# Decoder layer on one core: another deal of maxima, projections and context loads over the beats of the cross-attention

## The chip, the core and the metric

One core of one Trainium2 chip runs the kernel. The metric is the device time of one execution in microseconds; lower is better. TensorE (PE) does the matrix products and transposes, VectorE (DVE) the reductions and most element-wise work, ScalarE (ACT) exponentials and copies, GpSimd (POOL) sums and some DMA issues, SyncE (SP) only DMA issues.

## The reference, cut to what matters

`x` is 8 x 224 x 512, the context 8 x 750 x 512, all in float32. Three sublayers follow each other, each on the layer norm of the stream and added to it.

```
x = x + attn(layernorm(x), Wq, Wk, Wv, Wo, G1, G2, gamma, beta, theta)   # linear, causal, gated
x = x + xattn(layernorm(x), ctx, w_q, w_kv, w_proj, w_rel)
x = x + ffn(layernorm(x), w_gate, w_up, w_down)                          # ternary weights

# xattn: 16 heads of 32
q = x_q @ w_q ; k, v = split(ctx @ w_kv)
logits = q k^T * 32**-0.5 + (query position - key position) * w_rel[head]
out = softmax(logits) v  -> joined heads @ w_proj
```

The change touches the cross-attention alone.

## The kernel before, in words

The three sublayers run one after another: `self_attention`, `cross_attention`, `ternary_ffn`. Each engine has its own instruction stream, all written out in Python loops; semaphores join them. Engines take their instructions strictly in the order written, so the schedule is what the lists below say.

In `cross_attention` (L779) a batch has four slots, `s` = 0 to 3, one for each group of four heads. A slot has 16 beats `k`. What each engine does in a beat is written in fixed order:

- TensorE (L1371 to L1386): the maxima halves of the beat (`maxima_half`, L1311), at beat 12 `turn_maxima` (L1326), then the logits of a unit in beats 0 to 11 (`logits`, L1297: four heads for each of three pairs of key blocks), in beats 5, 9 and 13 a product with the values (`attend`, L1333), at beat 2 the denominators of the slot before (L1350), and last a part of a filler (`do`, L1235).
- Maxima: for the next slot (`n` is its number over all batches), each of 4 heads x 2 halves of the queries x 2 halves of the keys (376 columns) is one matmul into `psM`, which has two banks; VectorE reduces it (`reduce_half`, L1169). Half h goes to bank h % 2, so TensorE waits at half h for the reduction of half h - 2. After the last half VectorE joins them (`join_maxima`, L1179, at beat 11); TensorE turns the result at beat 12 and ScalarE copies it as the shift into `q4` (`take_shift`, L1089). `halves_at` (L806) says which halves lie in which beat: here 16 in beats 0 to 10.
- Fillers (`fill`, L815): projections and transposes that the slot has room for. K{g}a and K{g}b are the two halves of the keys of head group g, in three parts of four matmuls over three beats each; V{t} the values of key block t and Y{t} the output projection, three parts each; q{g} queries, r{t} the transposes of context block t, and Xa, Xb the transposes of x, in one beat each. Y belongs to the batch before, K2 and K3 to the batch itself, all others to the next one. V takes 12 matmuls of 512 columns, K 12 of 376, q 12 of 224, r and X four transposes.
- Each filler writes one of the two banks of `psR`, in turn (`bank_of`, L846 to L856, by the order of all fillers). The first part of a filler waits until the bank's filler before it has been read. Reading (`take` of ScalarE, L1061, and of VectorE, L1138) is put at the beat after a filler has ended: for K, r, X and q ScalarE copies the rounded high part and VectorE then subtracts it for the low part; V is only copied, Y only added. In VectorE's stream a beat's reductions stand ahead of its `take`, and at beat 2 both stand ahead of `divide` (L1183: reciprocal and product).
- SyncE packs keys and queries from `k_st` and `q_st` into `k4` and `q4` with DMAs (`pack_keys`, L932, 12 of them; `pack_queries`, L944). Keys of a group go over a buffer that the logits two slots earlier still read, so their four heads are packed behind beats 8 to 11. `k_st` is single: the copy of the next K{g}a (L1071) waits until all of the group before has been packed. The order of all this is fixed at L966 to L976.
- GpSimd, for each slot (L1036 to L1048): `split_heads` of the slot before (L996), in slot 0 of batches 1 to 6 the load of the next context (`load_context`, L1023, 1.5 MB by its own DMA queue), `store` in slot 1, `sum_keys` (L1008, five additions of 125 x 896 behind the exponentials), then `clear_shift` (L983). The context b goes into `cv[:, b % 2]` once the values of batch b - 2 have been used up (`pv_done`).

The kernel has two further pieces that matter for bounds: logits go to three banks, so the logits of a unit wait for the exponential of three units earlier (L1303), and all r of a batch must have been read before its K0a begins (L1244).

Of the kernel before, what the change touches and what calls it, by code (L numbers as in the profile page):

```python
# [19 lines left out]
NG = D // P  # L20
# [21 lines left out]
def wait_count(eng, sem, value):  # L42

    if not (isinstance(value, int) and value <= 0):
        eng.wait_ge(sem, value)


def wait_apart(eng, sem, value, passed):

    eng.wait_ge(sem, value)  # L50
    eng.sem_inc(passed, 1)
# [727 lines left out]
def cross_attention(nc, sems, x1, ctx_rows, k_rows, q_rows, x2, shared):  # L779
# [5 lines left out]
    B, N, _ = x1.shape  # L785
# [17 lines left out]
    BEATS = 16  # L803


    halves_at = [range(0, 1), range(1, 2), range(2, 4), range(4, 5), range(5, 7), range(7, 8), range(8, 10),  # L806
                 range(10, 11), range(11, 13), range(13, 14), range(14, 16)] + [range(0)] * 5
    unit_at = [(k // HG, k % HG) if k < UNITS else None for k in range(BEATS)]
    attend_at = {5: 0, 9: 1, 13: 2}
    DENOMINATORS_AT = 2  # L810
# [2 lines left out]

    parts_of = {"V": 3, "K": 3, "Y": 3, "q": 1, "r": 1, "X": 1}
    fill = [  # L815
# [4 lines left out]
    ]  # L820
    first_fill = ["r0", "r1", "r2", "r3", "r4", "r5", "K0a", "K0b", "Xa", "Xb", "q0", "q1", "K1a", "K1b", "q2", "q3"]
# [29 lines left out]
    bank_of, use_of, high_of = {}, {}, {}  # L851
# [6 lines left out]
    with ExitStack() as ctx:  # L858
# [42 lines left out]
        read = [sem("read_A"), sem("read_B")]  # L901
# [76 lines left out]
        @block.gpsimd  # L978
        def _(pool):
            nc.gpsimd.memset(eps_half[:], -0.5).then_inc(const_made, 1)  # L980
            pool.wait_ge(const_made, 1)

            def clear_shift(b, s):  # L983

                wait_apart(pool, st_full, UNITS * (NG * b + s + 1), pool_passed)
                nc.gpsimd.memset(q4[ROW_SHIFT:ROW_SHIFT + HG, s].bitcast(F32), 0.0).then_inc(shift_cleared, 1)
                pool.wait_ge(shift_cleared, NG * b + s + 1)

            def rstd(b):
                wait_apart(pool, x_meanvar, NT * (b + 1), pool_passed)  # L990
                nc.gpsimd.tensor_scalar(x_ve[:], x_mv[:, :, 1], EPS, None, ALU.add).then_inc(x_veps, 1)
                pool.wait_ge(x_veps, b + 1)
                nc.gpsimd.tensor_tensor(x_rs[:], x_ve[:], eps_half[:], ALU.pow).then_inc(x_rstd, 1)
                pool.wait_ge(x_rstd, b + 1)

            def split_heads(b, s):  # L996

                n = NG * b + s
                if s == 0 and b >= 1:
                    for what in ("Y0", "Y1"):  # L1000
                        wait_apart(pool, full[bank_of[what, b - 1]], use_of[what, b - 1], pool_passed)
                wait_apart(pool, o_ready, n + 1, pool_passed)
                nc.gpsimd.tensor_scalar(oT_hi[:, s], o_f[:], 1.0, None, ALU.mult).then_inc(oT_hi_ready, 1)  # L1003
                pool.wait_ge(oT_hi_ready, n + 1)
                nc.gpsimd.tensor_tensor(oT_lo[:, s], o_f[:], oT_hi[:, s].bitcast(F32), ALU.subtract).then_inc(oT_ready, 1)
                pool.wait_ge(oT_ready, n + 1)

            def sum_keys(b, s):  # L1008

                n = NG * b + s  # L1010
                wait_count(pool, den_full, n)
                for m in range(SUMS):
                    i, a = divmod(m + 1, 2)
                    tile = pT[:, (s + i) % 2, :, a * N:(a + 1) * N]
                    if m in (0, 1, 3):
                        wait_apart(pool, exp_done, UNITS * n + HG * (i + 1), pool_passed)
                    before = pT[:, s % 2, :, 0:N] if m == 0 else p_sum[:]
                    if m > 0:
                        pool.wait_ge(p_summed, SUMS * n + m)
                    nc.gpsimd.tensor_tensor(p_sum[:], before, tile, ALU.add).then_inc(p_summed, 1)  # L1020
                pool.wait_ge(p_summed, SUMS * (n + 1))

            def load_context(b):  # L1023

                wait_count(pool, pv_done, NB * NG * (b - 1))
                pool.dma_start(cv[:, b % 2], ctx_rows[b].rearrange("(a p) d -> p a d", p=KB)).then_inc(c_in, DMA)

            def store(b):
                for what in ("Y0", "Y1"):
                    pool.wait_ge(read[bank_of[what, b]], use_of[what, b])  # L1030
                pool.dma_start(x2_rows[b], x_res[:]).then_inc(stored, DMA)

            rstd(0)
            load_context(1)
            rstd(1)
            for b in range(B):  # L1036
                for s in range(NG):
                    if (b, s) != (0, 0):
                        split_heads(*((b, s - 1) if s > 0 else (b - 1, NG - 1)))
                    if s == 0 and b >= 1 and b + 1 < B:  # L1040
                        load_context(b + 1)
                    if s == 1 and b >= 1:
                        store(b - 1)
                    if s == 3 and b + 2 < B:
                        rstd(b + 2)
                    sum_keys(b, s)
                    if b + 1 < B:
                        clear_shift(b, s)  # L1048
            split_heads(B - 1, NG - 1)
            store(B - 1)  # L1050
            pool.wait_ge(stored, B * DMA)
# [180 lines left out]
        def _(pe):  # L1232
            M = nc.tensor

            def do(what, b, part):  # L1235

                r = bank_of[what, b]
# [4 lines left out]
                if what[0] == "K":  # L1242
                    g, seg = int(what[1]), "ab".index(what[2])
                    if g == 0 and seg == 0 and part == 0:  # L1244
                        for t in range(NK):
                            pe.wait_ge(read[bank_of[f"r{t}", b]], use_of[f"r{t}", b])
                    lo = seg * (S - SEG)
                    out = out[:, 0:SEG]
                    left = lambda i, k: (w_hi, w_lo)[i][:, 1, k, g * P:(g + 1) * P]
                    right = lambda i, k: (cT_hi, cT_lo)[i][:, k, lo:lo + SEG]  # L1250
                elif what[0] == "r":
                    t = int(what[1])
                    if t == 0:
                        wait_count(pe, c_in, DMA * b)
                    for k in range(KT):
                        last = M.transpose(out[:, k * KB:(k + 1) * KB], cv[:, b % 2, t, k * P:(k + 1) * P], ident[0:KB, 0:KB])
                    last.then_inc(full[r], 1)
                    return
                elif what[0] == "X":
                    seg = "ab".index(what[1])  # L1260
                    if seg == 0:
                        pe.wait_ge(xn_ready, NT * (b + 1))
                    for k in (0, 1):
                        for t in range(NT):
                            last = M.transpose(out[:, k * N + t * T:k * N + (t + 1) * T],
                                               xn[:, t, (2 * seg + k) * P:(2 * seg + k + 1) * P], ident[0:T, 0:T])
                    last.then_inc(full[r], 1)
                    return
                elif what[0] == "q":
                    g = int(what[1])  # L1270
                    for x_half in ("Xa", "Xb"):
                        pe.wait_ge(read[bank_of[x_half, b]], use_of[x_half, b])
                    out = out[:, 0:N]
                    left = lambda i, k: (w_hi, w_lo)[i][:, 0, k, g * P:(g + 1) * P]
                    right = lambda i, k: (xT_hi, xT_lo)[i][:, k, :]
                elif what[0] == "V":
                    t = int(what[1])
                    out = out[0:KB, :]
                    left = lambda i, k: (cT_hi, cT_lo)[i][:, k, t * KB:(t + 1) * KB]
                    right = lambda i, k: (w_hi, w_lo)[i][:, 2, k, :]  # L1280
                else:
                    t = int(what[1])
                    if part == 0:
                        pe.wait_ge(w_split_lo, 2)
                        pe.wait_ge(oT_ready, NG * (b + 1))
                    out = out[0:T, :]
                    left = lambda i, k: (oT_hi, oT_lo)[i][:, k, t * T:(t + 1) * T]
                    right = lambda i, k: (w_hi, w_lo)[i][:, 3, k, :]
                terms = [(i, j, k) for k in range(KT) for i, j in ((0, 0), (0, 1), (1, 0))]
                each = len(terms) // parts  # L1290
                for m in range(part * each, (part + 1) * each):
                    i, j, k = terms[m]
# [71 lines left out]
            for part in range(3):  # L1364
                do("V0", 0, part)
# [540 lines left out]
```

## Time and profile before

| | us |
|---|---|
| three runs | 1378.21, 1381.65, 2889.5 |
| their median | 1381.65 |
| the profiled execution | 1378.97 |
| its span, first to last instruction | 1377.4 |
| self-attention with its lead-in, from the start | 341.1 |
| cross-attention, from there to about | 1135 |

The profiled execution spends 1.57 us outside its span. The third of the three runs is far above the others and has no counterpart in the profile. The sections of the span were read from the first instruction of the cross-attention (341.10) and its last products (1128.56 and on).

In the timelines below a matmul's duration reaches past the start of the next one, since matmuls are pipelined; the distance between starts is what one takes of TensorE. Idle time in brackets is counted from the modelled end of the instruction before. Batches and slots are counted from 0.

### The profile page before, as it was taken

What the parts mean: (1) busy time and instruction counts of PE and PEld (TensorE: products, weight loads), DVE (VectorE), ACT (ScalarE), POOL (GpSimd) and SP (SyncE); (2) the same over time, 40 slices, a digit from 0 to 9 for tenths busy, and PEclk for the clock granted to TensorE, in tenths of its full rate; (3) what the DMA queues carried; (4) which work ended last, traced back from release to release, by engine and by line L of the source; (5) the groups of instructions that cost most, each with busy time, mean ns of one, the idle gap of its engine ahead of it and who ended that gap; (6) DMA issues with size and microseconds to landing.
All of it is one profiled execution on the core that took longest, in us unless ns stands there. A gap on an engine that the chain in (4) does not pass through costs nothing. (4 is left out here: it accounts for less than half of the span.)

```text
span 1377.4 us, 24731 instructions
## 1 busy us (share of the span) xinstructions
PE 1198.6 (87%) x9295; PEld 915.0 (66%) x9322; DVE 821.0 (60%) x1522; ACT 590.6 (43%) x955; POOL 515.8 (37%) x411
## 2 busy tenths in 40 slices
PE   4799989994689998999999989999999863599997
PEld 3687868882577777777777777777777643344443
DVE  5767646654356646465656465565654616688884
ACT  2222222231235444444444444454444324577775
POOL 0011111114006565656565646555655651001110
PEclk9899999997699999999999999999999855999999
DMA  5222242224413243344252532442423208212211
GB/s 159 87 74 86 77 139 96 82 90 137 124 47 102 51 131 94 77 118 101 63 144 55 126 102 68 118 105 60 120 74 87 61 0 327 84 54 69 69 61 38
DMA packets 72362, 129.42 MB, mean 94 GB/s; under 512 B 18572, under 2 KB 30988, under 8 KB 71739
## 3 DMA queue, kind: packets, MB, share of 16 engines
q1 hardware_dynamic: 60595, 106.43, 27.5%
q0 software_dynamic: 11680, 21.81, 5.0%
q8 instruction: 57, 0.93, 0.3%
q14 instruction: 30, 0.25, 0.1%
HBM read 68.96 MB, written 11.22 MB: 58 GB/s over the span
## 5 line engine op out<-in xcount | busy, mean ns | idle before, releaser
L1177 DVE TENSOR_REDUCE xa_m_part<-xa_psM 112x1 f32<-112x376 f32 x512 | 265.4, 544 | 258.9 <-PE xa_psM L1323 257.6
L1020 POOL TENSOR_TENSOR xa_p_sum<-xa_p_sum,space 125x896 f32<-125x896 f32 x128 | 270.1, 2110 | 124.0 <-ACT space L1101 118.6
L1101 ACT ACTIVATE space<-xa_psS 125x448 f32<-125x448 f32 x384 | 207.1, 544 | 237.0 <-PE xa_psS L1307 228.5
L1323 PE MATMUL xa_psM<-xa_k,xa_q 104*112 104x376 f32 x512 | 162.7, 356 | 21.8 <-DVE xa_m_part L1177 20.4
L1307 PE MATMUL xa_psS<-xa_q,xa_k 104*125 104x224 f32 x768 | 147.9, 278 | 0.0
L1307 PEld LDWEIGHTS xa_psS<-xa_q,xa_k 104*125 104x125 f32 x768 | 140.8, 194 | 8.2 <-issue 1.4
L1323 PEld LDWEIGHTS xa_psM<-xa_k,xa_q 104*112 104x112 f32 x512 | 89.6, 178 | 46.8 <-DVE xa_m_part L1177 32.8
L1345 PE MATMUL xa_psO<-space,cv 125*32 125x224 f32 x1536 | 97.9, 375 | 1.8 <-ACT space L1101 1.1
L1293 PE MATMUL xa_psR<-xa_cT_hi,w_hi 128*128 128x376 f32 x256 | 87.5, 342 | 9.7 <-DVE xa_cT_lo L1167 9.7
L1293 PE MATMUL xa_psR<-xa_cT_hi,w_lo 128*128 128x376 f32 x256 | 93.0, 363 | 0.0
L1293 PE MATMUL xa_psR<-xa_cT_lo,w_hi 128*128 128x376 f32 x256 | 86.5, 338 | 0.0
L60 PE MATMUL sa_psR<-sa_xT_hi,w_hi 128*128 128x224 f32 x256 | 72.8, 284 | 11.1 <-DVE sa_xT_lo L456 11.1
L1003 POOL TENSOR_SCALAR xa_oT_hi<-xa_o_f 128x224 fp32r<-128x224 f32 x32 | 24.7, 772 | 149.3 <-DVE xa_o_f L1190 149.3
L1293 PE MATMUL xa_psR<-w_hi,xa_cT_hi 128*125 128x512 f32 x192 | 78.2, 407 | 0.0
L1020 POOL TENSOR_TENSOR xa_p_sum<-space 125x896 f32<-125x896 f32 x32 | 67.6, 2112 | 27.4 <-ACT space L1101 23.4
L1293 PE MATMUL xa_psR<-w_lo,xa_cT_hi 128*125 128x512 f32 x192 | 77.3, 402 | 0.0
L1293 PE MATMUL xa_psR<-w_hi,xa_cT_lo 128*125 128x512 f32 x192 | 75.7, 394 | 0.0
L60 PE MATMUL sa_psR<-sa_xT_lo,w_hi 128*128 128x224 f32 x256 | 71.0, 277 | 0.0
L60 PE MATMUL sa_psR<-sa_xT_hi,w_lo 128*128 128x224 f32 x256 | 70.8, 277 | 0.0
L1056 ACT ACTIVATE xa_k_st<-xa_psR 128x376 fp32r<-128x376 f32 x64 | 30.9, 484 | 87.5 <-PE xa_psR L1293 65.7
L1807 PE MATMUL ff_psG<-ff_gu_T,ff_xq_T 128*128 128x512 bf16 x210 | 54.9, 380 | 13.6 <-DVE ff_h L1685 11.0
L1543 POOL DMA_DIRECT2D out_dram<-ff_y x14 | 8.7, 622 | 151.0 <-DVE ff_y L1700 151.0
(200 smaller groups left out, 2646.8 us busy)
## 6 DMA issues: line engine op xcount, KB each, us to landing
xa_k<-xa_k_st SPq DMA_DIRECT2D x384, 94.0 KB, 2.2
xa_q<-xa_q_st SPq DMA_DIRECT2D x192, 56.0 KB, 2.0
cv<-in_ctx_dram POOLq DMA_DIRECT2D x7, 1500.0 KB, 23.2
cv<-in_L_ffn_w_gate_dram SPq DMA_DIRECT2D x8, 512.0 KB, 4.9
cv<-in_L_ffn_w_up_dram SPq DMA_DIRECT2D x8, 512.0 KB, 6.1
cv<-in_L_ffn_w_down_dram SPq DMA_DIRECT2D x8, 512.0 KB, 7.1
ff_w_raw<-in_L_ffn_w_gate_dram SPq DMA_DIRECT2D x4, 1024.0 KB, 9.2
ff_w_raw<-in_L_ffn_w_up_dram SPq DMA_DIRECT2D x4, 1024.0 KB, 14.0
```

The lines of the kernel that those rows point to most:

```text
L60: ins = nc.tensor.matmul(out, left(i, c), right(j, c), start=first and n == 0, stop=last and n == len(terms) - 1)
L1003: nc.gpsimd.tensor_scalar(oT_hi[:, s], o_f[:], 1.0, None, ALU.mult).then_inc(oT_hi_ready, 1)
L1020: nc.gpsimd.tensor_tensor(p_sum[:], before, tile, ALU.add).then_inc(p_summed, 1)
L1056: return nc.scalar.activation(out, in_, ACT.Copy, scale=scale)
L1101: nc.scalar.activation(pT[:, (s + i) % 2, j], psS[0:KB, (HG * i + j) % NB, 0:2 * N], ACT.Exp).then_inc(exp_done, 1)
L1177: V.tensor_reduce(m_part[:, seg, t, jj:jj + 1], psM[0:T, seg, 0:SEG], AX.X, ALU.max, negate=True).then_inc(mx_read, 1)
L1293: last = M.matmul(out, left(i, k), right(j, k), start=m == 0, stop=m == len(terms) - 1)
L1307: last = M.matmul(psS[0:KB, (HG * i + j) % NB, a * N:(a + 1) * N], k4[0:ROWS, s % 2, j, col:col + KB], q4[0:ROWS, s, j, :], start=True, st ...
L1323: M.matmul(psM[0:T, seg, 0:SEG], q4[0:ROWS, g, jj, t * T:(t + 1) * T], k4[0:ROWS, g % 2, jj, seg * SEG:(seg + 1) * SEG], start=True, stop= ...
L1345: last = M.matmul(psO[HD * j:HD * (j + 1), 0:N], cv[:, b % 2, t, h * HD:(h + 1) * HD], pT[:, (s + i) % 2, j, a * N:(a + 1) * N], start=t == 0,
L1543: pool.dma_start(out_rows[i], y[:]).then_inc(stored, DMA)
L1807: last = M.matmul(bank[:, c % 2], xq_T[:, k], gu_T[:, w, k, c * CW:(c + 1) * CW], start=k == 0, stop=k == KT - 1)
```

## The change

It has four parts.

1. The 16 halves are dealt over twelve beats, 2, 1, 1, 1, 1, 1, 1, 2, 2, 1, 2, 1, in place of eleven beats with 1, 1, 2, 1, 2, 1, 2, 1, 2, 1, 2. The last half then stands in beat 11, in the beat of `join_maxima` and right ahead of `turn_maxima`.
2. The fillers are dealt otherwise. Y0 and the two X change places in slot 0, Y1 moves from beat 13 to 11; q2, q3 go from slot 0 to slot 2; in slot 1 r and q alternate and V0 takes beats 12 to 14; r4 and r5 move to slot 1's last beat and slot 2's beat 1; K0 moves from beats 0 to 5 of slot 2 to beats 3 to 8. Slot 3 stays. All in all the same fillers run; the banks follow from the new order.
3. The context of batch b + 2 is asked for at the end of slot 3 of batch b, behind `clear_shift`, in place of slot 0 of batch b + 1 between `split_heads` and `sum_keys`. There are six such loads either way.
4. The first part of a V waits for r{t} of its block to have been read, one wait more in TensorE's stream for each V.

```diff
--- before.py
+++ after.py
@@ -803,8 +803,8 @@
     BEATS = 16
 
 
-    halves_at = [range(0, 1), range(1, 2), range(2, 4), range(4, 5), range(5, 7), range(7, 8), range(8, 10),
-                 range(10, 11), range(11, 13), range(13, 14), range(14, 16)] + [range(0)] * 5
+    counts = (2, 1, 1, 1, 1, 1, 1, 2, 2, 1, 2, 1)
+    halves_at = [range(sum(counts[:k]), sum(counts[:k + 1])) for k in range(BEATS)]
     unit_at = [(k // HG, k % HG) if k < UNITS else None for k in range(BEATS)]
     attend_at = {5: 0, 9: 1, 13: 2}
     DENOMINATORS_AT = 2
@@ -813,9 +813,9 @@
 
     parts_of = {"V": 3, "K": 3, "Y": 3, "q": 1, "r": 1, "X": 1}
     fill = [
-        {0: "K2a", 3: "K2b", 6: "Xa", 7: "Xb", 8: "Y0", 11: "q2", 12: "q3", 13: "Y1"},
-        {0: "K3a", 3: "K3b", 6: "r0", 7: "r1", 8: "q0", 9: "r2", 10: "r3", 11: "q1", 12: "r4", 13: "r5"},
-        {0: "K0a", 3: "K0b", 6: "V0", 9: "V1", 12: "V2"},
+        {0: "K2a", 3: "K2b", 6: "Y0", 9: "Xa", 10: "Xb", 11: "Y1"},
+        {0: "K3a", 3: "K3b", 6: "r0", 7: "q0", 8: "r1", 9: "q1", 10: "r2", 11: "r3", 12: "V0", 15: "r4"},
+        {0: "q2", 1: "r5", 2: "q3", 3: "K0a", 6: "K0b", 9: "V1", 12: "V2"},
         {0: "K1a", 3: "K1b", 6: "V3", 9: "V4", 12: "V5"},
     ]
     first_fill = ["r0", "r1", "r2", "r3", "r4", "r5", "K0a", "K0b", "Xa", "Xb", "q0", "q1", "K1a", "K1b", "q2", "q3"]
@@ -1037,8 +1037,6 @@
                 for s in range(NG):
                     if (b, s) != (0, 0):
                         split_heads(*((b, s - 1) if s > 0 else (b - 1, NG - 1)))
-                    if s == 0 and b >= 1 and b + 1 < B:
-                        load_context(b + 1)
                     if s == 1 and b >= 1:
                         store(b - 1)
                     if s == 3 and b + 2 < B:
@@ -1046,6 +1044,8 @@
                     sum_keys(b, s)
                     if b + 1 < B:
                         clear_shift(b, s)
+                    if s == NG - 1 and b + 2 < B:
+                        load_context(b + 2)
             split_heads(B - 1, NG - 1)
             store(B - 1)
             pool.wait_ge(stored, B * DMA)
@@ -1275,6 +1275,8 @@
                     right = lambda i, k: (xT_hi, xT_lo)[i][:, k, :]
                 elif what[0] == "V":
                     t = int(what[1])
+                    if part == 0:
+                        pe.wait_ge(read[bank_of[f"r{t}", b]], use_of[f"r{t}", b])
                     out = out[0:KB, :]
                     left = lambda i, k: (cT_hi, cT_lo)[i][:, k, t * KB:(t + 1) * KB]
                     right = lambda i, k: (w_hi, w_lo)[i][:, 2, k, :]
```

## Rows read from the trace of the kernel before

**Rows 1.** The page: TensorE's busy time, and its granted clock in 40 slices
```profile
PE 1198.6 (87%) x9295; PEld 915.0 (66%) x9322; DVE 821.0 (60%) x1522; ACT 590.6 (43%) x955; POOL 515.8 (37%) x411
...
PEclk9899999997699999999999999999999855999999
```

**Rows 2.** Stretches: two batches of the cross-attention, each from reciprocal to reciprocal
```profile
core 0: us, PE busy (x) PEld busy (x) DVE busy (x) ACT busy (x) POOL busy (x), PEclk, DMA share, GB/s
...
586.30:678.90 92.60, 88.13 (x665) 71.22 (x666) 53.64 (x105) 41.54 (x78) 54.68 (x36) 1.00 0.38 97
...
678.90:770.80 91.90, 87.94 (x665) 71.33 (x666) 53.62 (x106) 41.67 (x79) 54.69 (x36) 1.00 0.38 99
```

**Rows 3.** TensorE's timeline, batch 2, slot 0 (start us, us, what; idle before and releaser)
```profile
583.89 0.34 PE L1323 MATMUL xa_psM<-xa_k,xa_q 104*112 104x376 f32 x1
...
584.28 0.34 PE L1293 MATMUL xa_psR<-xa_cT_lo,w_hi 128*128 128x376 f32 x1
...
584.98 0.51 PE L1323 MATMUL xa_psM<-xa_k,xa_q 104*112 104x376 f32 x2
...
588.02 0.34 PE L1323 MATMUL xa_psM<-xa_k,xa_q 104*112 104x376 f32 x1
...
588.78 0.43 PE L1323 MATMUL xa_psM<-xa_k,xa_q 104*112 104x376 f32 x1 [0.42 <-DVE xa_m_part L1177]
...
589.04 0.38 PE L1307 MATMUL xa_psS<-xa_q,xa_k 104*125 104x224 f32 x2
```

**Rows 4.** TensorE's timeline: the other waits of batch 2, and one pair of maxima
```profile
594.01 0.60 PE L1265 MATMUL xa_psR<-ident,xa_xn 112*128 112x112 f32 x4 [0.27 <-DVE xa_k_st L1167]
...
614.65 0.43 PE L1323 MATMUL xa_psM<-xa_k,xa_q 104*112 104x376 f32 x1 [0.53 <-DVE xa_m_part L1177]
...
618.80 0.65 PE L1256 MATMUL xa_psR<-ident,cv 125*128 125x125 f32 x4 [0.27 <-DVE xa_k_st L1167]
...
623.06 0.59 PE L1323 MATMUL xa_psM<-xa_k,xa_q 104*112 104x376 f32 x2
...
625.15 0.37 PE L1293 MATMUL xa_psR<-xa_xT_hi,w_hi 128*128 128x224 f32 x1 [0.65 <-DVE xa_cT_lo L1167]
...
630.33 0.41 PE L1293 MATMUL xa_psR<-xa_cT_hi,w_hi 128*128 128x376 f32 x1 [1.10 <-DVE xa_cT_lo L1167]
```

**Rows 5.** VectorE's timeline around three of these waits
```profile
586.28 1.56 DVE L1187 RECIPROCAL xa_den<-xa_psO 128x224 f32<-128x224 f32 x1
...
588.18 0.54 DVE L1177 TENSOR_REDUCE xa_m_part<-xa_psM 112x1 f32<-112x376 f32 x1
...
622.12 0.38 DVE L1164 SCALAR_TENSOR_TENSOR xa_q_st<-xa_psR,xa_q_st 128x224 fp32r<-128x224 f32 x1
...
623.51 1.01 DVE L1177 TENSOR_REDUCE xa_m_part<-xa_psM 112x1 f32<-112x376 f32 x2 [1.01 <-PE xa_psM L1323]
...
624.43 0.67 DVE L1167 TENSOR_TENSOR xa_cT_lo<-xa_psR,xa_cT_hi 128x500 fp32r<-128x500 f32 x1
...
625.01 0.15 DVE L1181 TENSOR_TENSOR xa_m_neg<-xa_m_part 112x8 f32<-112x8 f32 x1
```

**Rows 6.** ScalarE's timeline: the copy of K3a in batch 2
```profile
613.08 0.48 ACT L1056 ACTIVATE xa_k_st<-xa_psR 128x376 fp32r<-128x376 f32 x1 [2.79 <-DMA xa_k<-xa_k_st]
```

**Rows 7.** GpSimd's timeline at the boundary of batches 1 and 2
```profile
583.22 0.84 POOL L986 MEMSET xa_q<- 4x896 f32 x1 [0.18 <-POOL xa_p_sum L1020]
...
588.45 0.78 POOL L1003 TENSOR_SCALAR xa_oT_hi<-xa_o_f 128x224 fp32r<-128x224 f32 x1 [4.39 <-DVE xa_o_f L1190]
...
590.29 1.63 POOL L1026 DMA_DIRECT2D cv<-in_ctx_dram  x1 [0.30 <-ACT space L1101]
```

**Rows 8.** The DMA view, 500 to 620 us: the context's transfer
```profile
cv<-in_ctx_dram POOLq DMA_DIRECT2D x1, 1500.0 KB, 23.2
```

**Rows 9.** The DMAs that pack keys into k4, issued 580 to 620 us
```profile
DMA to landing us min/median/max: 2.3/3.0/10.5
```

**Rows 10.** SyncE's timeline: the last issues of K0's packing, slot 2 of batch 2
```profile
646.78 3.67 SPq L941 DMA_DIRECT2D xa_k<-xa_k_st  x6
```

## The prediction

> **What bounds the kernel now.** I read the page first, then stretches, then TensorE's waits in order of time, then for each wait the engine that ended it. TensorE is busy for 1198.6 of 1377.4 us, and its granted clock stands at nine tenths or above, but for the stretch ahead of the cross-attention and for that behind its middle [rows 1]. Two neighbouring batches of the cross-attention take 92.6 and 91.9 us at a clock of 1.00 (2.4 GHz); TensorE is busy for 88 us of each, POOL for 55, VectorE for 54 and ScalarE for 42 [rows 2]. So in batches 0 to 6 TensorE's stream sets the time, and only what shortens it or fills its gaps counts. The same instructions run after the change, so all that can go are the gaps.
>
> How dear is a gap? In batch 2, slot 0, half 5 starts at 588.02 and half 6 would follow 0.18 later, as half 2 and what follows it do; it starts at 588.78 and its logits 0.26 behind it instead of 0.18 [rows 3]. The row shows 0.42 idle, and 0.58 + 0.08 = 0.66 to 0.68 are lost: a wait costs its idle time plus about 0.26, since the matmul before it is modelled past its successor's start.
>
> The waits of one batch: (a) half 6 of each of four slots, 0.42 idle each, behind the reciprocal of 1.56 at 586.28 and the product, so that half 4's reduction starts only at 588.18 [rows 3, 5]; (b) Xb in slot 0 and r1 in slot 1 wait for K's low part, 0.27 each; (c) q1 waits 0.65 for r2's low part; (d) K0a waits 1.10 for that of r5 [rows 4]. That is 4 x 0.41 + 2 x 0.27 + 0.65 + 1.10 = 3.93 idle in 8 waits, so 3.93 + 8 x 0.26 = 6.0 us. (e) Half 7 of slot 1 waits another 0.53 (0.79 lost) at 614.65 [rows 4]. There ScalarE had stood 2.79 us until the packing of K2 had landed [rows 6]; such a wait on ScalarE comes in batches 1 to 5, and TensorE's behind it in four of them.
>
> **The deal of halves.** With one half in beat 2 and one in beat 4, half 6 moves to beat 5. A beat of K with one half is 584.98 - 583.89 = 1.09 long, of which four matmuls are 0.70 [rows 3]. Half 4 is reduced at 588.18 + 0.54; half 6 now comes a beat after 588.3. So (a) goes, 4 x 0.67 = 2.7. In its place the last half stands in beat 11 and the turn right behind it. Beat 11 is about 1.3 long with four matmuls of 512 columns (0.39 for half and logits by rows 3, and 512/376 of 0.70), the half needs about 0.45 to its reduction, 0.54 for it and 0.15 for the join [rows 3 to 5]: 1.14. In slots 2 and 3 that just fits, zero; half 11, in the second pair in a row, may wait 0.1.
>
> **The deal of fillers.** Slot 0: Y1 in beat 11 needs Xa's bank, Xa ended in beat 9, and two reductions lie ahead of Xa's low part. This is the pattern of (c): the pair starts at 623.06, the reductions at 623.51, the low part ends at 625.10, TensorE goes on at 625.15, so 2.09 behind the pair [rows 4, 5]. TensorE is ready after two halves and logits (0.56), Xb (0.65 less 0.2 of overlap [rows 4]) and half and logits (0.39): 1.40. Wait: 0.65 with X priced as r. The turn then hides behind Y1.
>
> Slot 1: q0 in beat 7 needs K3b, now behind one reduction instead of two: 0.1 left of 0.5. r3 in beat 11 needs q1's low part, 0.38 instead of 0.67 [rows 5]: 1.80 against 1.40, wait 0.40. Then the join (2.37) is late for the turn (2.25): 0.17. V0 in beat 12 needs r2's low part, queued behind the join: 2.37 + 0.67 + 0.05 against about 2.65: 0.4. (c) and r1's wait are gone. Slot 2: r4 has all of q2, and r5 all of q3 behind it before a bank or K0a needs them, so (d) is gone. (b) in slot 0 goes as well: Y0 takes K2a's bank, read long before, and Xa comes three beats after K2b. Behind the product (588.2) POOL has split the heads by about 590.1 [rows 7]; Y0 comes at about 591.5, uncovered only if POOL slips 1.4.
>
> Sum of new waits: 0.65 + 0.1 + 0.40 + 0.17 + 0.4 + 0.1 = 1.8, plus 0.08 for each of six restarts, 2.3. Waits of this sort that I haven't found are likely; I add 0.5. Bounds for the new waits: 0, if the reads come as early as they can, and 5.4, twice what I found plus as much again as the addition (2 x 2.3 + 0.8). I take 2.8: its terms come from rows of the same pattern. So a batch gives 6.0 - 2.8 = 3.2.
>
> The extra wait ahead of each V costs nothing: r0 has been read six beats before V0, r1 to r5 as long before theirs, and K0a waited for all r already. Behind TensorE's instruction nothing new is queued.
>
> **The context.** POOL's issue takes 1.63 and stood between head split and sum [rows 7]; POOL has 38 us to spare in a batch [rows 2], so this alone is worth nothing on TensorE's path. It now follows the memset that ends at 584.06, where POOL idles 4.39 until the head split [rows 7]. Its own wait, for the last product with the values (beat 13), is over by then. The transfer took 23.2 [rows 8], so from 590.3 to 613.5; it now ends about 607.4. The slowest of the key DMAs took 10.5 against a median of 3.0 [rows 9], and ScalarE's wait ended at 613.08, just ahead of the context's end [rows 6, 8]. The context's load then lies over the packing of queries too, which nobody needs for long. K3a's copy is due about 610.3, behind 607.4, so (e) goes: 0.8 in four batches, 3.2; bounds 0 (it stays) and 3.2.
>
> The row shows that key DMAs, of 2.3 us at best, land late beside the context. The Trainium skill (DMA: Bandwidth & Descriptors, Queues, rings and completion order) gives a reason: the completion increment lands only after every earlier write of that DMA engine, whatever the queue. By that rule K2's packing is freed when the context is, which the trace bears out within 0.5 us; without it, the gain of the context's part would be 0, and the sum 3.2 us higher.
>
> **Sum.** 7 batches x 3.2 = 22.4, and 3.2: 25.6. Batch 7 has few fillers and is bound by latency, entry and the other sublayers don't change: 0, with 2 either way. Against the profiled execution 1378.97 (its span and 1.57 around it): 1353.4, 1.9% less. The median of the runs shown is 2.7 higher; I keep to the profiled time.
>
> **Rivals.**
> - *The gaps go and few come* (0.2). TensorE pulls on as readers finish early; new waits half as dear, 1.4 a batch: 1353.4 - 7 x 1.4 = 1343.6. For it: VectorE and ScalarE are idle 39 and 51 us of a batch [rows 2] and can read early. Against: VectorE's order puts two reductions ahead of each low part.
> - *New waits for old* (0.22). The tail of slots 0 and 1 packs last half, join, turn and bank reads together; with 5.4 a batch and (e) staying: 1378.97 - 7 x 0.6 = 1374.8. For: five of the new waits lie there. Half-way is 1365.
> - *Slower: the packing of K0 becomes the bound* (0.05). K0b ends at beat 8 instead of 5, so the packing starts about 14.6 instead of 14.2 into slot 2; its 12 issues at 0.61 each [rows 10] end at 22, landing 2 to 3 later, and K1a's copy is due at about 26. Should each land as late as the slowest did (10.5 [rows 9]), it is 32.5: 6.5 late, of which some 5 would reach TensorE by the logits and products behind ScalarE: 1378.97 - 25.6 + 35 = 1388. It decides from 3.7 us a batch. Against: no context is in flight there, and every other term must hold.
> - *The context doesn't matter* (0.08): K2's packing lands late by itself; 1356.6.
>
> The forecast has 0.45 (1348 to 1360). Clock: no gap that I expect is over 0.7 us, and batches with gaps of 1.1 kept a clock of 1.00 [rows 2, 4]; a fall of some us costs about 1.
>
> **Chances.** A difference of 2% (about what a measurement of this kernel can tell from no change) is 27.6 us, 1351.4. Below lies most of the first rival (0.17) and a third of the forecast (0.15): faster 0.32. Slower by over 2% needs the slower rival at a higher price and a fall of the clock: 0.02. Same 0.66. Range 1341 to 1371: it takes in most of both neighbours and leaves out the slower case.
>
> **What would show it.** Right: a batch at 88.5 to 89.5 us by the stretches; no wait of half 6; none of K0a for a low part; waits of Y1 (about 0.4 idle) and r3, turn, V0 in slots 0 and 1 (0.1 to 0.4); the context's issue at the memset's end, and no DMA wait of the key copy. Wrong: batches above 91, waits of the turn in all slots, TensorE waiting for exponentials or for packed keys in slot 3, or a granted clock under 1.00 in batches 1 to 6.

## The result, and the profile after

The changed kernel takes 1366.46 us (median of 8 runs, 1361.6 to 1371.65) against 1380.08 for the one before; the ratio is 0.9914 with a 95% interval of 0.9897 to 0.993. By the ratio that is 12 us less (13.6 by the medians) where 25.6 were forecast: the right way, and about half of the size. It lies inside the stated range of 1341 to 1371, but on the side of the rival of new waits for old.

The profiled execution took 1367.56 us. The page's busy time and granted clock, answering to [rows 1]:

```profile
PE 1200.0 (88%) x9295; PEld 914.0 (67%) x9322; DVE 845.3 (62%) x1522; ACT 589.2 (43%) x955; POOL 517.4 (38%) x411
...
PEclk9999999998788999999999999999999965999999
```

TensorE is as busy as before, 1200.0 against 1198.6 us, in a shorter span. In the tenth to thirteenth slices, 307 to 444 us, the clock reads 8, 7, 8 and 8 tenths; before, it was low in the tenth and eleventh only. The stretches of batches 1 and 2, from reciprocal to reciprocal, answer to [rows 2]; their columns are those of the first row there:

```profile
499.16:588.81 89.65, 87.48 (x665) 70.71 (x666) 57.43 (x104) 41.38 (x78) 54.97 (x36) 1.00 0.38 100
...
588.81:679.98 91.17, 89.03 (x665) 71.28 (x666) 57.42 (x105) 41.38 (x78) 54.93 (x36) 0.98 0.39 99
```

Batches 1, 3 and 5 take 89.6 us and batches 2, 4 and 6 take 91.2, the latter at a clock of 0.98. The forecast was 88.5 to 89.5 for all. What TensorE waited for in batches 1 to 6 (total us, times, longest), in place of the waits of [rows 3, 4]:

```profile
PE xa_psM L1332 <- DVE xa_m_neg L1181: 8.3, 6, 1.4
...
PE xa_psR L1295 <- DVE xa_xT_lo L1167: 2.1, 6, 0.4
...
PE xa_psR L1295 <- DVE xa_cT_lo L1167: 1.4, 6, 0.2
```

None of the old waits is left in these batches: no half waits, no K0a, no r1, no q1. Y1 waits 0.35 and V0 0.24, near what was forecast. But the longest of all is one that the forecast put at nothing: in slot 0 the turn of the maxima (L1332) waits 1.38 us for the join. VectorE, GpSimd and TensorE at that place in batch 2:

```profile
601.71 0.54 DVE L1177 TENSOR_REDUCE xa_m_part<-xa_psM 112x1 f32<-112x376 f32 x1
...
602.28 2.08 DVE L1181 TENSOR_TENSOR xa_m_neg<-xa_m_part 112x8 f32<-112x8 f32 x1
```

```profile
602.25 4.26 POOL L1020 TENSOR_TENSOR xa_p_sum<-xa_p_sum,space 125x896 f32<-125x896 f32 x2 [1.36 <-ACT space L1101]
```

```profile
604.42 0.45 PE L1332 MATMUL xa_psM<-ident,xa_m_neg 112*4 112x112 f32 x2 [1.38 <-DVE xa_m_neg L1181]
...
605.09 0.63 PE L1295 MATMUL xa_psR<-w_hi,xa_oT_lo 128*112 128x512 f32 x1
...
605.52 0.63 PE L1295 MATMUL xa_psR<-w_hi,xa_oT_hi 128*112 128x512 f32 x1
```

The join, 112 x 8 numbers, takes 2.08 us, where the same instruction takes 0.15 in [rows 5]. GpSimd's addition started 0.03 us ahead of it. The last half was reduced at 602.25, and the same beat's exponential released GpSimd's last two additions at about the same moment. Behind the wait TensorE's matmuls of 512 columns start 0.43 apart instead of 0.23: the clock stands at its lower level (1.2 GHz) for 3.4 us.

```profile
604.50:607.90 3.40, 3.40 (x22) 1.66 (x21) 0.39 (x1) 0.91 (x1) 2.86 (x2) 0.51 0.88 225
```

This happens in batches 2, 4 and 6 and makes the 1.5 us between the two kinds. In batches 1, 3 and 5 the turn waits just as long (1.40 us in batch 1) and the clock stays at 1.00. In batch 0, where slot 0 has no Y1 to cover anything, the join cost more: the turn waited 2.90 us, and the stretch behind it ran at 0.64:

```profile
422.60:432.00 9.40, 7.29 (x45) 5.37 (x45) 4.70 (x6) 2.50 (x4) 4.96 (x3) 0.64 0.51 131
```

The context's load stands where it was expected, and ScalarE's copy of K3a waits for no DMA any more ([rows 6, 7] before):

```profile
585.96 0.85 POOL L986 MEMSET xa_q<- 4x896 f32 x1 [0.18 <-POOL xa_p_sum L1020]
...
587.11 1.63 POOL L1026 DMA_DIRECT2D cv<-in_ctx_dram  x1 [0.30 <-POOL xa_q L986]
```

### The profile page after: what moved, and what is told of

The parts are those of the page before. It is cut to its first block and busy times, and to the rows that moved or that the text cites. A ratio compares the mean times of both kernels' runs of the same rounds, so it can differ in the third digit from the quotient of the medians.

```text
span 1366.0 us, 24785 instructions
## 1 busy us (share of the span) xinstructions
PE 1200.0 (88%) x9295; PEld 914.0 (67%) x9322; DVE 845.3 (62%) x1522; ACT 589.2 (43%) x955; POOL 517.4 (38%) x411
## 3 DMA queue, kind: packets, MB, share of 16 engines
q1 hardware_dynamic: 60595, 106.43, 27.7%
## 5 line engine op out<-in xcount | busy, mean ns | idle before, releaser
L1325 PEld LDWEIGHTS xa_psM<-xa_k,xa_q 104*112 104x112 f32 x512 | 88.4, 178 | 28.7 <-DVE xa_m_part L1177 12.3
L1295 PE MATMUL xa_psR<-xa_cT_hi,w_lo 128*128 128x376 f32 x256 | 92.6, 362 | 0.0
L1809 PE MATMUL ff_psG<-ff_gu_T,ff_xq_T 128*128 128x512 bf16 x210 | 54.9, 380 | 13.6 <-DVE ff_h L1687 11.0
L1187 DVE RECIPROCAL xa_den<-xa_psO 128x224 f32<-128x224 f32 x32 | 49.8, 1555 | 24.5 <-PE xa_psO L1357 24.5
## 6 DMA issues: line engine op xcount, KB each, us to landing
cv<-in_ctx_dram POOLq DMA_DIRECT2D x7, 1500.0 KB, 21.5
```

Of the source, the lines that this page charges most:

```text
L1187: V.reciprocal(den[:], psO[:, DEN:DEN + N]).then_inc(den_ready, 1)
L1295: last = M.matmul(out, left(i, k), right(j, k), start=m == 0, stop=m == len(terms) - 1)
L1325: M.matmul(psM[0:T, seg, 0:SEG], q4[0:ROWS, g, jj, t * T:(t + 1) * T], k4[0:ROWS, g % 2, jj, seg * SEG:(seg + 1) * SEG], start=True, stop= ...
L1809: last = M.matmul(bank[:, c % 2], xq_T[:, k], gu_T[:, w, k, c * CW:(c + 1) * CW], start=k == 0, stop=k == KT - 1)
```

## The experiments

**Theory A** says that the join stands still for as long as GpSimd's addition runs, since it has two inputs in SBUF and the addition reads SBUF too. Its rival B says that the join's place holds it up, or the transfer of the context. The trace speaks against the transfer by itself: in batch 0 no context is in flight at 422.6 (the one before had landed at 373.1), and the join takes 2.07 us there as well. It also speaks against the kind of operation: VectorE's other tensor_tensor instructions in this stage take one input from PSUM and one from SBUF, and they aren't held up. The low parts of the context in batches 1 to 6 (count; min, median, max in ns):

```profile
L1167 DVE TENSOR_TENSOR xa_cT_lo<-xa_psR,xa_cT_hi x36: 665/669/680, 528.9 to 997.2; 128x500 fp32r<-128x500 f32 x36
```

Twelve of these 36 lie wholly inside an addition of GpSimd, and none of them takes over 0.68 us.

**The join over one operand** (e1_join, on the changed kernel). The two parts lie side by side, and one reduction takes both.

```diff
-V.tensor_reduce(m_part[:, seg, t, jj:jj + 1], psM[0:T, seg, 0:SEG], AX.X, ALU.max, negate=True)
+V.tensor_reduce(m_part[:, t, jj, seg:seg + 1], psM[0:T, seg, 0:SEG], AX.X, ALU.max)
-V.tensor_tensor(m_neg[:], m_part[:, 0], m_part[:, 1], ALU.min)
+V.tensor_reduce(m_neg[:], m_part[:], AX.X, ALU.max, negate=True)
```

> The changed kernel, with the join of the two maxima parts written as one reduction over a single SBUF operand instead of a tensor_tensor of two. Theory A (the join of slot 0 stands still because a VectorE instruction with two SBUF inputs can't run beside GpSimd's addition, which reads SBUF too): the join takes at most 0.6 us in every slot instead of 2.08 in slot 0, the turn's wait of 1.38 us goes, no stretch of batches 1 to 6 shows a clock under 1.00, a batch takes about 88.0 us instead of 89.6 and 91.2, in all 1345 to 1352 us. Rival B (the join is held up by something that its operands have no part in: the place behind the last half, the transfer of the context): the join still takes 2 us in slot 0 and the time stays at 1364 to 1370 us.

Measured: 1352.85 us, ratio 0.9827 (0.9801 to 0.9852). VectorE and GpSimd at the same place, then the stretches of batches 1 and 4:

```profile
593.99 0.54 DVE L1177 TENSOR_REDUCE xa_m_part<-xa_psM 112x1 f32<-112x376 f32 x1
...
594.57 0.17 DVE L1181 TENSOR_REDUCE xa_m_neg<-xa_m_part 112x8 f32<-112x16 f32 x1
```

```profile
594.54 4.29 POOL L1020 TENSOR_TENSOR xa_p_sum<-xa_p_sum,space 125x896 f32<-125x896 f32 x2 [1.36 <-ACT space L1101]
```

```profile
492.53:581.10 88.57, 87.38 (x665) 70.75 (x666) 55.62 (x105) 41.13 (x78) 54.94 (x36) 1.00 0.39 101
...
757.62:845.70 88.08, 87.31 (x665) 70.76 (x666) 55.52 (x105) 41.36 (x78) 54.95 (x36) 1.00 0.39 103
```

The meeting is the same, GpSimd's addition starts 0.03 ahead of the join, but the join takes 0.17. All 32 joins take 0.17, the clock is 1.00 in batches 1 to 6, and a batch takes 88.1 to 89.0. Place and transfers were left as they were, so B falls. The meeting cost the changed kernel 14 us by the medians, 12 by the ratios. The forecast of 1353.4 is met once it is away. The time is 0.85 over the band of A; slot 1 now waits for packed keys in four batches (1.9 us in all, up to 1.0).

**Half as long additions** (e2_short_sums, on the changed kernel).

```diff
-nc.gpsimd.tensor_tensor(p_sum[:], before, tile, ALU.add).then_inc(p_summed, 1)
+for js in (slice(0, 2), slice(2, HG)):
+    nc.gpsimd.tensor_tensor(p_sum[:, js], before[:, js], tile[:, js], ALU.add).then_inc(p_summed, 1)
```

The waits for `p_summed` count double.

> The changed kernel, with each of GpSimd's additions cut in two of half the size (about 1.05 us each). Theory A (held for one whole GpSimd instruction): the join of slot 0 takes 1.0 to 1.1 us instead of 2.08, the turn's wait falls from 1.38 to about 0.35, in all 1354 to 1361 us. Rival B: the join stays at 2.08 us, 1366 us or, for the added instructions, somewhat more.

Measured: 1357.16 us, 0.9847 (0.9821 to 0.9873). The join, and GpSimd's (now 448 columns each, three of them in the row):

```profile
597.15 1.13 DVE L1182 TENSOR_TENSOR xa_m_neg<-xa_m_part 112x8 f32<-112x8 f32 x1
```

```profile
597.12 3.46 POOL L1021 TENSOR_TENSOR xa_p_sum<-xa_p_sum,space 125x448 f32<-125x448 f32 x3 [1.09 <-ACT space L1102]
```

1.13 instead of 2.08: the join's length follows that of a single addition, not of the sum of them. The turn's wait fell to 0.44 in this batch, and no clock fell in batches 1 to 6. A is shown by two edits that have nothing in common.

**The parts one by one.** Halves alone, fillers alone (with the wait ahead of V) and the context alone, each on the kernel before, are the corresponding hunks of the diff.

> The kernel before with the new deal of halves alone. By the prediction the four waits of half 6 go, 2.7 us a batch, 19 us in all: 1360 us. By theory A the last half and the join in beat 11 meet GpSimd's addition behind the exponential of beat 11 in slot 1, where r2's low part holds VectorE up: the join takes about 2 us there, the turn waits 1 to 1.8 us, and 4 to 12 us of the 19 are left: 1367 to 1375 us. Slot 0 with the old fillers has nothing on VectorE in beat 10, so no long join there.

Measured: 1368.48 us, 0.9939 (0.9916 to 0.9961). All joins of this kernel (min, median, max in ns):

```profile
L1181 DVE TENSOR_TENSOR xa_m_neg<-xa_m_part x32: 166/168/2066, 402.8 to 1087.8; 112x8 f32<-112x8 f32 x32
```

There the long join is that of slot 1, as A said: 2.05 us at 620.93 in batch 2, with 0.94 idle for the turn behind it, while slot 0's takes 0.17. The batches take 90.3 to 90.9 us and the clock stays at 1.00. So a meeting follows from the last half's beat and from what VectorE has to do ahead of it; of these two deals of fillers each only chose the slot.

> The kernel before with the early context alone. By the prediction ScalarE's wait for the packing of K2 and half 7's wait behind it go, 0.8 us in four batches: 1373 to 1377 us where before is 1377 to 1380. Under 5 us in any case; if it were worth 10 or more by itself, theory C would be wrong in making its gain depend on the new fillers.

Measured: 1376.19 us, 0.9975 (0.9955 to 0.9994): 3.4 us by the ratio (its interval says 0.8 to 6.2) and 1.3 by the medians, against 3.2 in the sum. ScalarE waits for no packed keys in batches 1 to 6 any more, half 7's wait is gone, and each of these batches takes 91.9 us; before, it was 92.6 or more in four of them and 91.9 in two.

> The kernel before with the new deal of fillers and the wait ahead of V alone. By the prediction's steps (b), (c) and (d) go, 3.3 us a batch, and waits of Y1, r3 and V0 come, about 1.3 with their restarts; the halves end in beat 10, so the join lies a beat ahead of the turn and nothing waits for it. 7 x 2.0 = 14 us less: 1361 to 1368 us. If the new waits are what ate the gain, under 5 us less.

Measured: 1394.7 us, 1.0111 (1.0084 to 1.0138). This was a plain miss: 15 us slower by the ratio (17 by the medians) instead of 14 faster. TensorE's waits over batches 1 to 6, the longest of them in slot 1 of batch 5, and the landing times of the key DMAs between 580 and 618 us:

```profile
PE xa_psM L1325 <- DVE xa_m_part L1177: 15.7, 28, 2.3
...
PE xa_psM L1325 <- DMA xa_k<-xa_k_st: 9.1, 6, 3.2
```

```profile
898.73 0.65 PE L1325 MATMUL xa_psM<-xa_k,xa_q 104*112 104x376 f32 x1 [3.24 <-DMA xa_k<-xa_k_st]
```

```profile
DMA to landing us min/median/max: 2.0/2.8/10.7
```

The maxima of slot 1 wait up to 3.2 us for K2's packed keys, others follow behind the late copy of K3a (up to 2.3 us), and the clock falls in four batches. Slot 0 has given q2 and q3 away and is some 2.5 us shorter (in batch 2, from reciprocal to reciprocal, 24.0 before and 21.5 with these fillers and no wait for keys), so slot 1 asks for the keys that much earlier, while they land beside the context. Some 9 of the 15.7 us are the old deal's own waits of half 6, about 0.4 each.

**Theory C** says that the transfer of the context is what makes K2's keys late, so that the early context is worth little alone and much with the new fillers. **Rival D** puts it down to the new fillers as such, **rival E** to the load of x behind the keys.

> The changed kernel with the old deal of halves: new fillers and early context together. Theory C (the new fillers shorten slot 0, so that slot 1 asks for K2's packed keys while they still land beside the context's transfer; the early context takes that transfer out of their way): no wait of over 0.5 us for packed keys, ScalarE's copy of K3a waits at most 2 us, and no long join, since the join stands a beat before the turn: 1358 to 1366 us, so 30 us under the fillers alone (1394.7), though the early context alone is worth at most 3 us. Rival D (the new fillers themselves are slow, by bank reads or by the x load that shares the keys' queue, wherever the context is): 1385 us or more.

The edit is the diff's hunk of the halves undone. Measured: 1370.52 us, 0.9946 (0.9925 to 0.9967), 4.5 us over the band. The early context takes 24 us off the fillers' 1394.7, where it takes 1.3 (by medians) off the kernel before. D, which asked for 1385 or more, falls. Some of the wait is left: up to 0.88 us in four batches, more than the 0.5 expected.

**No context at all** (e5_no_context, on the fillers alone).

```diff
-if s == 0 and b >= 1 and b + 1 < B:
-    load_context(b + 1)
...
-wait_count(pe, c_in, DMA * b)
+wait_count(pe, c_in, DMA * min(b, 1))
```

> The kernel with the new fillers alone, and the contexts of batches 2 to 7 not loaded at all (their keys and values are made of what the buffer holds, so the output is another; the instructions of the compute engines stay). Theory C (the keys of K2 land late because the context's transfer is in flight): no wait for packed keys in slot 1 and no key DMA over 4 us from issue to landing, 1358 to 1368 us, about 30 us under the 1394.7 with the loads. Rival E (the load of x, 0.4 MB, issued on the same queue right behind the keys, is what holds them): waits of 1 us and more stay, 1385 us or more.

Measured: 1368.33 us, 0.9927 (0.9906 to 0.9948), no wait for packed keys. The landing times of the keys, and the load of x (KB, us to landing):

```profile
DMA to landing us min/median/max: 2.1/2.2/2.8
```

```profile
xa_xn<-x_dram SPq DMA_DIRECT2D x1, 448.0 KB, 3.7
```

The slowest key DMA lands after 2.8 us instead of 10.7, with the load of x in its place; that load itself takes 3.7 instead of 10.5. The time is 26 us under the 1394.7, and 0.3 over the band. The transfer is shown as the cause of the late keys, and E falls.

> The changed kernel with the context asked for in slot 0 again, as before. Theory C: slot 1 waits 1 to 3 us for packed keys or for the copy of K3a behind them in every batch 1 to 6, as with the fillers alone, and the clock falls behind some of these waits: 1380 to 1392 us, 15 to 25 us over the changed kernel. Rival D: no difference, 1364 to 1370 us. The long join of slot 0 stays under both.

Measured: 1370.46 us, 0.994 (0.9918 to 0.9962). This missed too: 4 us over the changed kernel, not 15 to 25, and by its number nearer to D. The mechanism of C is there even so. ScalarE's copy of K3a in batch 4, and what TensorE waited for in batches 1 to 6 (total us, times, longest):

```profile
798.50 0.48 ACT L1056 ACTIVATE xa_k_st<-xa_psR 128x376 fp32r<-128x376 f32 x1 [4.89 <-DMA xa_k<-xa_k_st]
```

```profile
PE xa_psO L1347 <- ACT space L1101: 6.6, 4, 2.5
...
PE xa_psM L1325 <- DMA xa_k<-xa_k_st: 0.2, 1, 0.2
```

The copy waits 2 to 5 us in five of the six batches. The maxima hardly wait: slot 0 is longer by its own wait for the join, so the keys have landed more often when slot 1 asks, and with one half in beats 3 to 5 none queues behind the late copy. But the exponentials stand behind that copy in ScalarE's stream, and in four batches the product with the values waits for them, 0.8 to 2.5 us. A batch takes 91.1 us on average against 90.4 in the changed kernel, with one fall of the clock in batches 1 to 6 instead of three. So part of what the long join costs is, as I read it, time that the keys would have cost; no run separates the two.

> The changed kernel with the old fillers, so the new halves and the early context together. The halves alone gave 1368.5, the early context alone 1.3 us: 1364 to 1369 us, about the changed kernel's own 1366.5, whose fillers then gave nothing as long as their slot 0 pays for the long join. If the new fillers carry the change, 1372 us or more.

Measured: 1365.59 us, 0.9914 (0.9892 to 0.9935): the changed kernel's own time. As long as the join meets the addition, the new fillers give nothing. What they give without the meeting is not shown: no run has the old fillers with the join over one operand.

The table has the medians and, in brackets, the ratios to the kernel before. Its runs come from several sessions, in which the kernel before took 1377.2 to 1380.1 us, so a difference of 3 us or less between cells of different sessions isn't shown.

| | old fillers | new fillers |
|---|---|---|
| old halves, context late | 1377.5 (1) | 1394.7 (1.011) |
| old halves, context early | 1376.2 (0.998) | 1370.5 (0.995) |
| new halves, context late | 1368.5 (0.994) | 1370.5 (0.994) |
| new halves, context early | 1365.6 (0.991) | 1366.5 (0.991) |

**Control** (e0_join): the join over one operand, in the kernel before.

> Control: the kernel before with the join over one operand. There the join met GpSimd's addition once, for 0.9 us in the last batch, so the form by itself is worth at most 1.5 us: 1375 to 1378 us. Were it worth 5 us or more here, the gain of the join's run on the changed kernel would not be the meeting's in beat 11.

Measured: 1377.05 us, 0.9999 (0.9985 to 1.0013). The form alone is worth nothing that can be measured. (In the kernel before the join met an addition twice, not once: 0.41 us in batch 0 as well.)

**A second deal of halves** (e3_best): e1_join's kernel with `counts = (2, 1, 1, 1, 1, 1, 1, 2, 2, 2, 1, 1)`.

> The changed kernel with the join over one operand and the halves dealt 2, 1, 1, 1, 1, 1, 1, 2, 2, 2, 1, 1, so that a single reduction stands ahead of Xa's low part in slot 0 and of q1's in slot 1. From 1352.85 of the join's run: the waits of Y1 (0.35 idle), r3 (about 0.3) and half of V0's (0.24) go, 0.8 us a batch with their restarts: 1345 to 1349 us. If these waits only move on to the pair in beat 9, no change: 1351 to 1355 us.

Measured: 1348.8 us, 0.9788 (0.9749 to 0.9827), 29 us under the kernel before and 4 under e1_join, with intervals that overlap. Y1's wait and that for the packed keys, in batch 2:

```profile
593.12 0.49 PE L1295 MATMUL xa_psR<-w_hi,xa_oT_hi 128*112 128x512 f32 x1 [0.20 <-DVE xa_xT_lo L1167]
...
598.11 0.61 PE L1325 MATMUL xa_psM<-xa_k,xa_q 104*112 104x376 f32 x2 [0.67 <-DMA xa_k<-xa_k_st]
```

Y1 waits 0.20 instead of 0.35, V0 as long as before, and the wait for packed keys grows from 1.9 to 3.5 us over the six batches. The number lies in the band, but not for the reason given. These are batches 1 to 6 together and then batch 7, for this kernel:

```profile
492.58:1022.55 529.97, 523.45 (x3985) 423.61 (x3986) 329.69 (x619) 248.33 (x469) 326.74 (x213) 1.00 0.39 101
1022.55:1091.82 69.27, 56.92 (x428) 39.62 (x428) 33.44 (x62) 27.67 (x52) 48.39 (x29) 0.84 0.20 52
```

and batch 7 of e1_join, whose batches 1 to 6 take 530.56:

```profile
1023.09:1095.26 72.17, 61.08 (x428) 41.93 (x428) 33.76 (x62) 27.91 (x52) 48.37 (x29) 0.77 0.19 49
```

So the six batches give 0.6 us where 4.8 were expected. Most of the rest, 2.9, lies in batch 7, which ran at a clock of 0.84 instead of 0.77. That the second deal is better than e1_join's is not shown. **Earlier still** (e4_early) moves the context ahead of `clear_shift` in that kernel.

> The run with the join over one operand and the halves' second deal, with the context asked for ahead of the clearing of the shift instead of behind it, 1.15 us earlier. Slot 1's wait for K2's packed keys (0.67 to 1.03 us in four batches) and ScalarE's for K3a's copy shrink by up to 1.15: 1344 to 1348 us against 1348.8. If the keys' landing hangs on the bandwidth they share and not on the context's end: no change, 1347 to 1351 us.

Measured: 1351.73 us, 0.9813 (0.9788 to 0.9839), no gain: slot 1 waits 3.1 us for packed keys in batches 1 to 6 instead of 3.5. 1.15 us of head start don't free the keys; whether they share the engines' time with the context or have their completion held by it stays open.

## Why the prediction was wrong, point by point

- *The bound and the price of a wait.* Right. With the long join away a batch takes 88.4 on average (530.56 us for six), just under the 88.5 to 89.5 forecast.
- *The four waits of half 6, and (b), (c), (d).* Right; all are gone.
- *Y1, r3, V0 and slot 1's turn.* Right, in start against start: Y1 about 0.6 late where 0.65 was due, V0 0.4 for 0.4, and the turn of slot 1 0.17 for 0.17. r3 starts at 626.39 and could have started at about 626.11, 0.28 late against 0.40. Of the 0.5 a batch added for waits not found, none was needed in batches 1 to 6.
- *The turn.* The step that failed: "the half needs about 0.45 to its reduction, 0.54 for it and 0.15 for the join", and for slot 0 "the turn then hides behind Y1". The 0.15 was read where GpSimd wasn't adding. With GpSimd's addition running it is 2.08, and Y1's part can't hide it: 1.38 idle, 1.64 lost in each of six batches, with the clock's fall behind it three more times 1.5, and about 4 in batch 0 (from the first join to the first reciprocal it is 27.7 us, in e1_join 23.5). That is 18.5. The stretches differ by 16, in part since e1_join waits 1.9 us for packed keys again, and the medians by 14. The profile before had it already, in the last batch:

```profile
1083.40 0.90 DVE L1181 TENSOR_TENSOR xa_m_neg<-xa_m_part 112x8 f32<-112x8 f32 x1
```

```profile
1082.20 2.08 POOL L1020 TENSOR_TENSOR xa_p_sum<-xa_p_sum,space 125x896 f32<-125x896 f32 x1
```

The join ends with the addition, after 0.90 us instead of 0.17. A minimum and a maximum of the join's duration would have shown it. The Trainium skill has the rule (SBUF — State Buffer, Who interferes with whom): a VectorE instruction with two SBUF inputs contends with a GpSimd instruction that reads SBUF, for a shared pair of ports that is "an exclusive lock". The traces agree: 2.08, 1.13 and 0.17 us for an addition of 2.1, of 1.1 and for one input. The new deal moved the join to the beat whose exponential releases GpSimd, and the forecast looked only at VectorE's queue. The rival of new waits for old had the place, the tail of slots 0 and 1 with last half, join and turn together, but no long join either.
- *The context.* Its own worth, 3.2, fits (3.4 by the ratio, 1.3 by the medians), and the waits that it was to take away are gone. That it "doesn't matter" by itself was right only for the old fillers. With the new ones and the old halves it is worth 24 us, with the new halves 4; the sum treated the parts as independent. The slower rival had the right mechanism, packed keys that land late, but at K0 instead of K2, and saw no case in which it decides. It is K2's, in slot 1, and it decides in the run with the fillers alone.
- *Clock.* Wrong in that no fall was foreseen, and in its ground, that batches with gaps of 1.1 kept a clock of 1.00: [rows 2, 4] are of batches 2 and 3. In batch 4 of the same trace the clock fell for 3.4 us behind two waits of 0.41 and 1.03, and the batch took 94.7 us:

```profile
797.28 0.43 PE L1323 MATMUL xa_psM<-xa_k,xa_q 104*112 104x376 f32 x1 [0.41 <-DVE xa_m_part L1177]
...
799.63 0.43 PE L1323 MATMUL xa_psM<-xa_k,xa_q 104*112 104x376 f32 x1 [1.03 <-DVE xa_m_part L1177]
```

```profile
800.20:803.60 3.40, 3.40 (x23) 2.37 (x23) 0.44 (x1) 0.64 (x2) 1.44 (x1) 0.51 0.39 122
```

In the changed kernel it fell in three batches of six behind Y1's 0.35 and the turn's 1.38. The runs don't show why there and not in the other three, with the same waits.

Measured against the steps: 25.6 were forecast; with the join over one operand the ratio gives 24, and the meeting takes back 12 of them (14 by the medians, 1366.46 to 1352.85). The other 12 are the result.

## What to carry to other kernels

When a small VectorE instruction is moved, ask what GpSimd does at its new place as well as what stands ahead of it in its own queue. If it has two SBUF operands, give it one (a reduction over both parts here), or keep it clear of GpSimd's long additions; look at the maximum duration of such an instruction, not at its mean. And parts of a change that shift when a resource is asked for (packed keys) and when it is free (the transfer beside them) have to be judged together: by the medians the new fillers alone lost 17 us, the early context alone gave 1, and both with the old halves gave 7.

## What was not expected of the hardware

A join of 8 columns took 2.08 us beside a GpSimd addition of 896 columns, 1.13 beside one of 448, and 0.17 with a single SBUF input beside the same addition. A key DMA of 94 KB took up to 10.7 us from issue to landing beside a transfer of 1.5 MB on GpSimd's queue, and at most 2.8 without it. A wait of TensorE of 1.4 us, with one of 0.35 shortly before, was followed by the lower clock for 3.4 us in three batches of six, and one of 1.03 with 0.41 before it once in the kernel before.
